# Storing the expert outputs of a macaron block from ScalarE's queue, one transfer per tile

## The reference

```python
x = x + 0.5 * _L0_ffn_ref(_layernorm(x), gate_w, expert_bias, w1, w2, w3)
x = x + _L0_attn_ref(_layernorm(x), Wq, Wk, Wv, Wo)      # 16 heads of 8, softmax over 256 keys
x = x + 0.5 * _L0_ffn_ref(_layernorm(x), gate_w, expert_bias, w1, w2, w3)

# _L0_ffn_ref, 8 experts, hidden 352, two per token
scores = jax.nn.softmax(xf @ gate_w.T, axis=-1)
_, sel = jax.lax.top_k(scores + expert_bias, TOP_K)
...
routed = xf[token_idx] * top_scores_sorted[:, None]       # rows sorted by expert
h = jax.nn.silu(xe @ w1[e]) * (xe @ w3[e])
out = out + h @ w2[e] * m
...
out = jnp.zeros_like(xf).at[token_idx].add(routed_out)
```

## Time and profile before

| | us |
|---|---|
| median of 3 runs | 1022.8 (1018.39 to 1027.21) |
| profiled execution | 1022.84 |
| its span | 1021.0 |
| mean granted clock of PE | 0.824 |
| PE busy | 681.1 (67%) |
| DVE busy | 498.0 (49%) |
| ACT busy | 376.0 (37%) |
| POOL busy | 297.8 (29%) |
| result stores, all on SP's queue | 64 of 128 KB and 28 of 64 KB |

### The profile page before, as it was taken

The page is one execution under the profiler, slowest core; times in us unless marked ns, Lnnn a source line. Parts: engine busy times, 40 slices in busy tenths (PEclk is TensorE's granted clock), DMA queues, the critical chain, the costliest instruction groups (busy, mean ns, idle before and its releaser), DMA issues. The chain is left out here.

```text
span 1021.0 us, 14686 instructions
## 1 busy us (share of the span) xinstructions
PE 681.1 (67%) x4966; PEld 495.1 (48%) x4966; DVE 498.0 (49%) x1286; ACT 376.0 (37%) x862; POOL 297.8 (29%) x309
## 2 busy tenths in 40 slices
PE   5065786954797348888987777447769868279900
PEld 5044676853696113444443333223658757268800
DVE  2842483220354247888778789331438622015301
ACT  0211632311243016657675754346354223114400
POOL 4037304466503720010001000520232155560065
PEclk9978798885798558889998797879779979679955
DMA  5134663644472715423434331212247456346532
GB/s 189 41 114 120 177 189 107 171 140 103 141 205 81 195 33 134 125 80 90 131 91 127 109 98 56 53 19 89 60 135 211 119 144 186 79 135 180 142 100 71
DMA packets 105273, 121.80 MB, mean 119 GB/s; under 512 B 11184, under 2 KB 87472, under 8 KB 104944
## 3 DMA queue, kind: packets, MB, share of 16 engines
q1 hardware_dynamic: 87664, 98.05, 33.4%
q0 software_dynamic: 9088, 18.63, 7.5%
q10 hardware_dynamic: 8448, 4.20, 1.3%
HBM read 89.37 MB, written 31.20 MB: 118 GB/s over the span
## 5 line engine op out<-in xcount | busy, mean ns | idle before, releaser
L526 POOL DMA_INDIRECT xe<-normed_rows,idx x156 | 149.0, 955 | 308.7 <-DVE idx L438 193.9
L925 DVE TENSOR_REDUCE mx<-banks 128x2 f32<-128x512 f32 x256 | 164.0, 685 | 47.3 <-PE banks L806 23.7
L845 ACT ACTIVATE PT<-banks 128x512 f32<-128x512 f32 x256 | 141.4, 604 | 84.6 <-PE banks L817 62.2
L683 DVE TENSOR_TENSOR hidT<-banks,act 96x256 f32<-96x256 f32 (+1 forms) x92 | 34.8, 378 | 269.9 <-ACT act L654 210.4
L621 PE MATMUL banks<-WR,hidT 128*128 128x128 f32 x936 | 128.3, 287 | 37.2 <-issue 34.9
L539 POOL DMA_INDIRECT rows<-slots_out,slot x128 | 122.2, 955 | 99.7 <-DMA slots_out<-ye 61.9
L599 PE MATMUL banks<-xeT,WR 128*128 128x256 f32 (+1 forms) x368 | 96.7, 390 | 76.2 <-issue 75.6
L621 PEld LDWEIGHTS banks<-WR,hidT 128*128 128x128 f32 x936 | 119.9, 203 | 41.9 <-issue 39.9
L804 PE MATMUL banks<-KS,QS 56*128 56x256 bf16 x256 | 73.3, 302 | 63.2 <-DVE mx L925 40.8
L498 POOL TENSOR_TENSOR rough<-var,half_power 128x16 f32<-128x16 f32 x6 | 17.6, 2926 | 306.8 <-DVE var L258 306.8
L599 PEld LDWEIGHTS banks<-xeT,WR 128*128 128x128 f32 x368 | 64.9, 211 | 84.7 <-issue 80.3
(11 more groups left out here) (160 smaller groups left out, 956.3 us busy)
## 6 DMA issues: line engine op xcount, KB each, us to landing
WR<-in_experts SPq DMA_DIRECT2D x92, 544.0 KB
stacks<-split SPq DMA_DIRECT2D x32, 384.0 KB
slots_out<-ye SPq DMA_DIRECT2D x64, 128.0 KB
QS<-stacks SPq DMA_DIRECT2D x64, 112.0 KB
KS<-stacks SPq DMA_DIRECT2D x64, 112.0 KB
normed_rows<-xn ACTq DMA_DIRECT2D x16, 256.0 KB, 2.3
xe<-normed_rows,idx POOLq DMA_INDIRECT x156
rows<-in_xt SPq DMA_DIRECT2D x2, 1024.0 KB, 9.3
```

Of the source, the lines that this page charges most:

```text
L526: eng.indirect_dma_start(xe[:, i % XR, a, :], None, normed_rows[h], bass.IndirectOffsetOnAxis(ap=idx[h][:, tile:tile + 1], axis=0))\
L845: eng.activation(PT[:, u % 4, 1 - k].rearrange("p t n -> p (t n)"), PS[f % 3], ACT.Exp, scale=scale).then_inc(s_exp2, 1)
L925: eng.tensor_reduce(mx[:, :, e, pair], PS[3 + e][:, :].rearrange("p (q n) -> p q n", q=2), AX.X, ALU.max).then_inc(s_max, 1)
```

## The change

`rows_out` moves from SP's program to ACT's. It issues one transfer of 128 rows (64 KB) for each tile, so two for a pair, where a pair was one transfer of 128 KB. In round i ACT issues the stores of load i - 2, between Silu of load i (L654) and the copy of turned rows (L643); the last load's stores come after the loop. Since a pair now adds 32 to its `s_st`, the waits count tiles, by the new `stored`.

```diff
+        def stored(i):
+
+            return 16 * sum(load_of(k)[2] for k in range(i % RING, i + 1, RING))
...
                 for r in range(RING):
-                    eng.wait_ge(s_st[r], 16 * len(range(r, (g + 1) * NL, RING)))
+                    eng.wait_ge(s_st[r], stored((g + 1) * NL - 1 - (((g + 1) * NL - 1 - r) % RING)))
...
         def expert_sync(eng, first, last):
-            lag = 2
-
             def weights(i):
...
-            def rows_out(i):
-                g, l, w, row = load_of(i)
-                eng.wait_ge(s_ye, i + 1)
-                eng.dma_start(slots_out[g % HALVES][row:row + w * P, :].rearrange("(a p) d -> p a d", a=w),
-                              ye[:, i % RING, 0:w, :]).then_inc(s_st[i % RING], 16)
-
-            for i in range(first, last + lag + 2):
-                if i < last:
-                    weights(i)
-                if i - lag - 2 >= first:
-                    rows_out(i - lag - 2)
+            for i in range(first, last):
+                weights(i)
...
         def expert_scalar(eng, first, last, *sides):
 
+            def rows_out(i):
+                g, l, w, row = load_of(i)
+                eng.wait_ge(s_ye, i + 1)
+                for a in range(w):
+                    eng.dma_start(slots_out[g % HALVES][row + a * P:row + (a + 1) * P, :], ye[:, i % RING, a, :])\
+                       .then_inc(s_st[i % RING], 16)
+
...
+                if i > first + 1:
+                    rows_out(i - 2)
                 if i + 1 < last:
                     turned(i + 1)
                 if i > first:
                     g, l, w, row = load_of(i - 1)
                     r = (i - 1) % RING
                     eng.wait_ge(s_y, i)
-                    wait(eng, s_st[r], 16 * ((i - 1) // RING))
+                    wait(eng, s_st[r], stored(i - 1 - RING))
                     eng.copy(ye[:, r, 0:w, :].rearrange("p a d -> p (a d)"), PS[1][:, 0:w * D]).then_inc(s_ye, 1)
                 aside(sides, i)
+            rows_out(last - 1)
```

## The result

The changed kernel takes 1026.2 us (median of 20 runs, 1018.2 to 1031.9) and the kernel before, on the same chip and between those runs, 1021.6 us (median of 20, 1007.4 to 1029.6). The ratio is 1.0076, with a 95% interval of 1.0050 to 1.0101. That ratio goes by fast runs alone, and ten of the 20 runs of the kernel before lie more than 1.5% above its fastest, the mark of a slow run, while none of the changed kernel does; the medians of all 20, given above, are 4.7 us or 0.46% apart. The forecast was 1023.2 us with a range of 1009 to 1036 us, and a change of less than 1% had a chance of 0.68; the measured time lies in both. The interval excludes 1, however, and the forecast had priced the change at 0.3 us. So the question of what follows is whether those 0.46 to 0.76%, 5 to 8 us, belong to the change.

A forecast was written before the change was run, and what follows sets the result against it. Outside unexplained standstills, PE was taken to bound the expert loop. Terms 0 + 0 + 0 + 0.3 us on the profiled 1022.84 us, agreeing with the 1022.8 us median, gave 1023.2 us, range 1009 to 1036 us.

The forecast's parts named there:

- no change: Whole kernel: 1023.2 us forecast, a difference within about 1% (10 us) of the kernel before, chance 0.68.
- SP's 92 issues: SP in the expert stages: losing 92 store issues of 0.43 us gains 0, since SP was idle there.
- ACT's 156 issues: ACT between L654 and L643: a pair's 0.84 to 0.96 us fits covers of 1.08 and 1.26 us; term 0.
- the first rival's second form: ACT becomes PE's bound in type 0 loads, its issues also sitting out SP's: 9 us more, 1036 to 1040 us; chance 0.07.
- The end: Last store ahead of POOL's final gathers: two issues instead of one, +0.3 us, bounds -0.5 to +1.9 us.
- Late stores: Stores in the expert stages: later issue and shorter landing about cancel for POOL's gathers; term 0, bounds -1 to +3 us.
- mark of an error: Expert stages differing from 517 us by more than 6 us, with standstills and period unchanged, would show the forecast wrong.
- Rivals 2 and 3: PE's 110 us of expert-stage standstills: fewer, 1006 or 1012 us, chance 0.18; or more, 1040 us, chance 0.11.

The follow-up runs named there:

- e7: e1 timed once more: changed kernel with a pair's store as one whole transfer on ACT; 864.8 us, ratio 1.0010 to the kernel before.
- e8: Changed kernel with a pair stored as one whole transfer on ACT, moved behind L643; 861.7 us, ratio 1.0008 to the kernel before.
- e1: Changed kernel with the split undone: stores on ACT in the same place, one transfer for a pair; 861.0 us, ratio 0.9934 to the kernel before.
- e4: Changed kernel with each tile stored in two transfers of 64 rows, four for a pair; 916.3 us, ratio 1.0597 to the kernel before.
- e9: Changed kernel with each tile stored in two transfers of 128 rows and half the columns; 1051.7 us, ratio 1.0315 to the kernel before.
- e3: Changed kernel with each store right behind the copy that makes it, two loads earlier; 866.3 us, ratio 1.0017 to the kernel before.
- e12: Changed kernel with its stores, still split and on ACT, moved behind L643; 1020.8 us, ratio 1.0025 to the kernel before.
- e6: Kernel before timed against itself, no edit; 863.7 us, ratio 1.0039.
- e2: Kernel before with the split alone: SP stores in its old place, one transfer per tile; 864.5 us, ratio 1.0007 to the kernel before.
- e11: Kernel before timed against itself again, no edit, on a chip where it takes some 1020 us; 1019.8 us, ratio 1.0008.
- e5: Changed kernel timed again, no edit, on a chip with hardly any standstills; 866.5 us, ratio 1.0025 to the kernel before.
- e10: Changed kernel timed a third time, no edit, on a chip like the prediction's; 1020.0 us, ratio 0.9992 to the kernel before.

## Why the prediction was right

**The forecast, "no change".** Three comparisons of the same change gave 1.0076, 1.0025 and 0.9992, two of the kernel before with itself 1.0039 and 1.0008. A loss of up to some 0.5% can't be excluded; none was shown, and the first interval isn't evidence of one: the next comparison on the same kind of chip has it the other side of 1, and part of the 0.76% is the choice of runs, since all runs give 0.46%.

**SP's 92 issues, 0.** Right: with whole transfers moved from SP to ACT (e7, e8) the ratios are 1.0010 and 1.0008, their intervals within 0.5% of 1; e1's 0.9934 is the same kernel as e7 and did not repeat. The Trainium skill (DMA: Bandwidth & Descriptors, Issuing engines are not separate DMA queues) says that another issuing engine saves time in issuing alone; e7 and e8 agree, and since that time was idle on SP, nothing is left to save.

**ACT's 156 issues, 0 behind a cover of 1.08 and 1.26 us.** Right in place and in kind, and this is the step that the case turns on. I took the cover from L654's start and not from its end, 1.08 and not 0.70 us, because of the earlier trace rows. The timeline after shows the issues 0.00 to 0.01 us behind L654's start, the pair over in 0.81 us, L643 released by PE as before, and the period at 10.49 us. Had the issues waited for L654's end, 0.81 us would have been 0.11 too long for the 0.70. e4 and e9 show from the other side that the cover is real and about as large as read: at 1.98 us of issues PE's weight loads idle 1.00 us, and at 2.40 us 1.42 us. The price of a pair came out right, but in part by luck. In type 2, from the first issue's start to L643's, it is 946.42 - 945.52 = 0.90 us, inside the 0.84 to 0.96 of the sum. The sum took each issue as 0.37 to 0.43 us and 0.05 us to the next instruction; they are 0.33 and 0.45 us, with 0.03 us between them and 0.09 behind. I had read SP's 0.43 us as the price of its queue, and it is the price of an issue right behind another.

**The exceptions.** I had allowed for SP's issues falling into ACT's window, 9 us in the first rival's second form. The traces speak against that form: issues of both queues run side by side, and neither gets longer. At 918 us of the changed kernel's trace (the pair's row stands in the last section) SP's issue lies inside the pair of ACT, which takes its usual 0.81 us:

```profile
918.27 0.33 SPq L569 DMA_DIRECT2D WR<-in_experts  x1
```

In e3, where the stores stand behind the copy of `ye`, 84 issues of ACT overlap one of SP's loads of weights, and 82 of them take 0.33 to 0.35 us, the loads 0.33 to 0.35 us too. Long issues do occur, eight of 156, and one of them cost PE 0.60 us. The Trainium skill (Perfetto Trace Analysis, the per-instruction lifecycle) counts the wait for the descriptor generator's lock into an issue's window, so it allows such lengths; a wait of one queue for the other, which the prediction drew from the same section, is not what these overlaps show. What does go with them is another transfer. The profile's table of DMA queues for 968.6 to 970.7 us of the same trace, where the longest issue lies, has the row (packets, MB, share of 16 engines)

```profile
q8 instruction: 1, 0.02, 4.1%
```

a packet of the kind that the profile calls "instruction", 16 KB. In the fourteen traces together (the two kernels and e1 to e12, from 57 us on) such a packet is under way during 82 of the 132 store issues above 0.6 us (0.7 in e4), and during 134 of the 1980 others; in e6 during all eight long ones. They go together far more often than chance would have it, but no run here was made to show that one causes the other, and 50 long issues have no such neighbour. The long issues come to some 6 us on ACT in all, mostly where PE is not held by it, and on SP (e2, up to 1.50 us) too.

**The end, +0.3 us.** Not settled. In the traces it went from 3.12 to 4.79 us, near the upper bound of +1.9. But the same stretch is 4.73 and 4.68 us in the traces of the kernel before in the two controls, and 4.95 and 3.46 us in the two repetitions of the changed one. The spread of 3.1 to 5.0 us is in both kernels; a term of 0.3 us can't be read from one trace, and +1.9 has no support either: the six traces with whole stores (before, e1, e6, e7, e8, e11) have 4.0 us in the mean, the six with two for a pair (the changed kernel, e2, e3, e5, e10, e12) 4.3 us.

**Late stores, 0 (-1 to +3 us).** The stretches agree with it: 517.6 against 517 us with "issue" waits 4 us shorter, inside the 6 us that I had named as the mark of an error. The mark was too fine for one trace, though: in e11, the kernel before again, the two stages take some 8 us less than in the first trace of it. e3, with each store right behind its copy (1.0017), is no faster than e2 (1.0007) or e5 (1.0025), so no cost of their lateness can be seen.

**Rivals 2 and 3, standstills fewer or more.** Both refuted. They didn't move with the stores: 106.2 us against 110.3, and in the repetition e10 they come to 105 us (30.8 + 24.0 + 9.8 + 37.6 + 3.0). The name can change. In e11, the kernel before, 77 us are called "issue" and another 35 us "ACT ye", the longest of them 15.8 us. And e10's 9.8 us stand where the other traces name DVE; the second row is that of the changed kernel's first trace:

```profile
PE banks L582 <- issue: 9.8, 1, 9.8
...
PE banks L582 <- DVE xe L675: 8.6, 1, 8.6
```

With "ACT ye" counted in all four and this place in none, the two traces of the kernel before have 113 and 112 us, those of the changed one 115 and 114. They do move with the chip. PE's waits of the kernel before on the chip of e6, first expert stage and second:

```profile
PE banks L599 <- issue: 4.2, 1, 4.2
...
PE banks L604 <- DVE hidT L683: 19.3, 5, 9.4
PE banks L599 <- issue: 5.5, 3, 4.5
```

That is 9.7 us of "issue" where it was 110.3 for the same instructions; the changed kernel has 10.1 us there (e5). Busy time of the same kernel by stretch (expert stage, attention, expert stage; columns as in the earlier trace rows):

```profile
57.00:254.00 197.00, 173.01 (x1134) 154.46 (x1134) 102.34 (x308) 81.77 (x204) 111.98 (x112) 0.96 0.71 199
254.00:602.00 348.00, 274.92 (x2597) 139.02 (x2597) 258.10 (x581) 205.94 (x434) 56.34 (x55) 0.86 0.38 106
602.00:809.00 207.00, 180.95 (x1134) 160.52 (x1134) 97.06 (x280) 81.77 (x204) 89.08 (x91) 0.92 0.61 172
```

The expert stages take 404 us in place of 517, at a granted clock of 0.96 and 0.92 in place of 0.83 and 0.86, and attention 348 in place of 397. Of these 113 us of the expert stages, 86 are PE's waits under every name (136 us before, 50 us in e6, where "DVE hidT" grew) and 27 are PE's own busy time, 381 against 354 us, at the higher clock. The 49 us of attention I did not take apart. What starts the standstills is open: the large ones come at the same loads in every trace of this kind of chip, with the stores whole on SP, or on ACT split in two or in four. No "instruction" packet is under way in the longest (866.7 to 884.1 us of the kernel before). No run here was aimed at their cause.

None of the variants beats the two kernels in a result that repeats, so there is no better version to give.

## What to carry to other kernels

Before moving an issue to another engine, take the gap there from the start of the instruction ahead to the one behind, find who ends that gap, and set the sum of the issues against it: 0.81 us in 1.08 us cost nothing, 1.98 us cost 1.00. Read the price of an issue where it stands as yours will, alone or right behind another. When the effect expected is below 1%, time the kernel before against itself as well; here that alone gave 1.0039 with an interval that excluded 1. Look at the medians of all runs beside a ratio of chosen ones. And repeat a surprising ratio before explaining it: both of this case, 1.0076 and 0.9934, went away.

## What was not expected of the hardware

- A store of 64 rows of 512 bytes takes longer to issue from ACT (0.45 us alone, 0.62 behind another) than one of 128 rows (0.33 and 0.45). The same bytes in 128 rows of 256 have a median of 0.453, with the first of a group at 0.33.
- Two issues in a row: 0.33 us for the first, 0.45 for the second. SP is no slower: 0.33 us for a load of weights, 0.43 for the store right behind it, 0.36 for a whole store alone. Issues of SP and ACT that overlap in time keep these lengths (84 places in e3).
- Of the rare issues above 0.6 us, on either queue, 82 of 132 have a packet of the kind "instruction" under way beside them, of the others 134 of 1980.
- An issue can start ahead of the instruction that stands before it in ACT's program:

```profile
917.97 0.81 ACTq L636 DMA_DIRECT2D slots_out<-ye  x2
...
918.39 0.37 ACT L654 ACTIVATE act<-banks 96x256 f32<-96x256 f32 x1
```

  The issues begin 0.42 us before L654, which is ahead of them in the program: L654, not yet started, did not hold them up.
- One program takes 863 us on one chip and 1020 us on another, and most of the difference in the expert stages (86 of 113 us) is time in which PE waits, the larger part of it with no releaser that the profile can name.
